# A two-batch transformer block on one core: where the q and k scales are made, when GpSimd scales the last residual, and which engines normalise the last tiles

## Time and profile before

| | |
|---|---|
| median of 3 executions | 521.55 us (521.29 to 521.72) |
| the profiled execution | 521.81 us, its span 519.7 us |
| mean granted TensorE clock | 0.998 of full speed |
| TensorE, busy | 501.1 us of the span (96%), 2976 matmuls |
| VectorE, busy | 413.0 us (79%) |
| ScalarE, busy | 405.5 us (78%) |
| GpSimd, busy | 255.7 us (49%) |
| DMA | 29.20 MB, mean 56 GB/s |
| chain that ended last, by engine | PE 79%, DVE 7%, POOL 5%, ACT 5%, issue 2%, DMA 1% |

### The profile page before, as it was taken

The page is one execution under the profiler, slowest core; times in us unless marked ns, Lnnn a source line. Parts: engine busy times, 40 slices in busy tenths (PEclk is TensorE's granted clock), DMA queues, the critical chain, the costliest instruction groups (busy, mean ns, idle before and its releaser), DMA issues.

```text
span 519.7 us, 8086 instructions
## 1 busy us (share of the span) xinstructions
PE 501.1 (96%) x2976; PEld 193.2 (37%) x2976; DVE 413.0 (79%) x705; ACT 405.5 (78%) x558; POOL 255.7 (49%) x295
## 2 busy tenths in 40 slices
PE   8899999999999999999999999999999999999994
PEld 3222222323222322234444444444444444444441
DVE  3699999989999997368878778778668666788677
ACT  1522888998899989877888888888888888888880
POOL 9100091823100715073464676664997962648741
PEclk9999999999999999999999999999999999999999
DMA  6410018576530005700031121140020020000022
GB/s 192 136 68 5 21 35 211 182 144 125 91 59 1 3 5 103 276 7 1 1 59 24 20 43 21 20 62 1 1 81 1 0 83 0 3 0 1 0 81 81
DMA packets 30151, 29.20 MB, mean 56 GB/s; under 512 B 19489, under 2 KB 21921, under 8 KB 29857
## 3 DMA queue, kind: packets, MB, share of 16 engines
q1 hardware_dynamic: 26688, 22.67, 15.7%
q0 software_dynamic: 3424, 6.03, 6.3%
HBM read 24.37 MB, written 4.23 MB: 55 GB/s over the span
## 4 chain that ended last, share of the span: by engine, by line
PE 79%; DVE 7%; POOL 5%; ACT 5%; issue 2%; DMA 1%; SPq 0%; DVEq 0%; POOLq 0%; ACTq 0%
PE ps L1123 16%; PE ps L1135 16%; PE ps L1157 16%; PE ps L1068 9%; PE ps L1039 6%; PE ps L963 6%; DVE mxh L1249 4%; ACT pbuf L760 3%; PE ps L892 3%; POOL x L617 2%; PE ps L1051 1%; PE ps L902 1%; PE ps L1016 1%; POOL stack L663 1%; DMA arena<-xT 1%
## 5 line engine op out<-in xcount | busy, mean ns | idle before, releaser
L1249 DVE TENSOR_REDUCE mxh<-ps 128x1 f32<-128x512 f32 x256 | 157.0, 680 | 6.5 <-PE ps L963 5.3
L760 ACT ACTIVATE pbuf<-ps,gamma 128x1024 f32<-128x1024 f32 x128 | 140.5, 1114 | 16.2 <-PE ps L1039 11.2
L841 ACT ACTIVATE ps<-ps,ratio 128x512 f32<-128x512 f32 x168 | 106.5, 659 | 40.4 <-PE ps L1123 37.3
L1157 PE MATMUL ps<-wd,stack 128*128 128x512 f16 x440 | 129.7, 379 | 0.7 <-POOL stack L663 0.6
L1123 PE MATMUL ps<-arena,wg 128*128 128x512 f16 x448 | 115.5, 379 | 0.1
L1135 PE MATMUL ps<-arena,wu 128*128 128x512 f16 x448 | 115.3, 379 | 0.1
L1423 DVE TENSOR_TENSOR ps<-ps,stack 128x512 f32<-128x512 f32 x128 | 87.8, 695 | 33.4 <-PE ps L1157 31.7
L847 ACT ACTIVATE ps<-ps,ratio 128x512 f32<-128x512 f32 x156 | 98.9, 659 | 6.6 <-PE ps L1135 2.3
L661 POOL CAST stack<-pbuf 128x512 f16<-128x512 f32 x55 | 33.5, 609 | 76.5 <-DVE pbuf L1398 76.5
L1423 DVE TENSOR_TENSOR ps<-ps,pbuf 128x512 f32<-128x512 f32 x76 | 52.6, 695 | 23.2 <-PE ps L1157 22.5
L1068 PE MATMUL ps<-pbuf,arena 128*32 128x256 f32 x832 | 66.5, 391 | 1.7 <-ACT avt L767 1.7
(11 more groups left out here) (120 smaller groups left out, 387.4 us busy)
## 6 DMA issues: line engine op xcount, KB each, us to landing
arena<-xT SPq DMA_DIRECT2D x16, 256.0 KB, 5.8
x<-x SPq DMA_DIRECT2D x2, 2048.0 KB, 10.0
out<-x SPq DMA_DIRECT2D x3, 1024.0 KB, 4.2
stack<-down_ratios SPq DMA_DIRECT2D x1, 2048.0 KB, 9.6
wg<-gq POOLq DMA_DIRECT2D x4, 448.0 KB, 7.3
wu<-uq POOLq DMA_DIRECT2D x4, 448.0 KB, 7.4
wd<-dq POOLq DMA_DIRECT2D x2, 896.0 KB, 10.3
pbuf<-down_ratios SPq DMA_DIRECT2D x1, 1536.0 KB, 6.2
```

Of the source, the lines that this page charges most:

```text
L760: nc.scalar.activation(pbuf[:, pi % 4, :].rearrange("p (a n) -> p a n", a=2), ps[:, at:at + 2, :], ACT.Exp, scale=gamma[:, n // (ALL // B) ...
L841: nc.scalar.activation(gbank[t % 2], gbank[t % 2], ACT.Copy, scale=gr[:, t % G, c:c + 1])\
L1157: mm = nc.tensor.matmul(bank[k], mparts[:, a, t % NM, k * P:(k + 1) * P], wd[:, i, :], start=(i == 0 and a == 0), stop=(a == 1), skip_grou ...
L1249: nc.vector.tensor_reduce(mxh[:, f % 2, qh, half:half + 1], ring_bank("first", n), AX.X, ALU.max)\
```

## The change

It has three parts.

1. *Scales.* For batch 0, VectorE takes the maxima straight from PSUM, before the bias is added, and adds the bias's absolute value to the combined maxima (a bound on the biased values instead of their maximum). ScalarE's eviction of a bank waits for VectorE's maxima of that bank. The maxima are turned by four matmuls that give the row on all 128 partitions at once (own kind first on each half), after the first value piece instead of the second; `scale_row` works on all partitions and writes `unit` and `gamma` itself, and `cast_scales` and `place_scales` go, for batch 1 as well, and with them one ring use. The first q rows are kept by VectorE instead of ScalarE. VectorE clears the first half of `vst` between the two maxima, GpSimd the second half after the low parts.
2. *Residual.* The ten multiplications stand at periods 26, 27, 33, 34, 35 and 40 to 44.
3. *The last tiles.* GpSimd negates the means of tiles 0 and 1; ScalarE subtracts them from PSUM and multiplies by the inverse deviation in a second instruction; it does that multiplication for tile 3 too, after VectorE has subtracted the mean, and issues that tile's store itself. VectorE does tile 2 whole.

```diff
-        row = sb("row", [1, 8], F32)
+        row = sb("row", [P, 4], F32)
...
-        TOPS_AT = {(2, 1): "tops", (4, 1): "cast"}
+        TOPS_AT = {(2, 1): "tops"}
...
-        RESIDUAL_AT = 28
+        RESIDUAL_AT = (26, 27, 33, 34, 35, 40, 41, 42, 43, 44)
...
-            for i, k in enumerate(LAST_ORDER):
+            def store_last(k):
                 t = BT * (NB - 1) + k
-                sp.wait_ge(s_res, BT * (NB - 1) + i + 1)
                 sp.dma_start(out[t], x1[:, t, :]).then_inc(s_out, 16)
+            for k in range(2):
+                sp.wait_ge(s_resa, k + 1)
+                store_last(k)
+            sp.wait_ge(s_res, BT * (NB - 1) + 1)
+            store_last(2)
...
+            pool.wait_ge(s_low, 2)
+            nc.gpsimd.memset(arena[:, 3, :], 0.0).then_inc(s_zero1, 1)
+            pool.wait_ge(s_zero1, 1)
+            nc.gpsimd.memset(vst[1][:, :, :, E:E + 1], float(HD) ** 0.5).then_inc(s_zero1, 1)
...
+            for k in range(2):
+                pool.wait_ge(s_st, 2 * NB + k)
+                nc.gpsimd.tensor_scalar(negm[:, k:k + 1], mv[:, k, 0:1], -1.0, None, ALU.mult).then_inc(s_neg, 1)
             inverse(2 * NB - 1, slice(0, 2), 2 * NB + 1)
             inverse(2 * NB, slice(2, 4), 2 * NB + 3)
...
-                act.wait_ge(s_proj, (1, 2, 4, 6)[2 * b + k])
+                if b == 0:
+                    act.wait_ge(s_top, k + 1)
+                else:
+                    act.wait_ge(s_proj, (4, 6)[k])
...
-                act.wait_ge(s_unit, 3)
+                act.wait_ge(s_projr, 2)
+                act.wait_ge(s_row, 4)
...
-            for n in range(3):
-                keep(n)
+            keep(0)
+            keep(2)
             project_v(0)
...
+            def centre(k):
+                act.wait_ge(s_neg, k + 1)
+                nc.scalar.activation(x1[:, (NB - 1) * BT + k, :], bank[k], ACT.Identity, bias=negm[:, k:k + 1])\
+                  .then_inc(s_cent, 1)
+            def scale_result(k):
+                x1_t = x1[:, (NB - 1) * BT + k, :]
+                act.wait_ge(s_rstd, 2 * NB + k // 2)
+                if k < 2:
+                    act.wait_ge(s_cent, k + 1)
+                else:
+                    act.wait_ge(s_cent3, 1)
+                nc.scalar.activation(x1_t, x1_t, ACT.Copy, scale=rstd[:, k:k + 1]).then_inc(s_resa, 1)
+            for k in range(2):
+                centre(k)
+            for k in (0, 1, 3):
+                scale_result(k)
+            act.wait_ge(s_resa, 3)
+            act.dma_start(out[NB * BT - 1], x1[:, NB * BT - 1, :]).then_inc(s_out, 16)
...
-                return [(qk, k, c) for k in range(2) for c in range(C)] + [(v, 0), (v, 1), (turn_tops, 0, bank[3]), (v, 2),
-                                                                           (cast_scales, 0, bank[3]), (v, 3), (vt,)]
+                return [(qk, k, c) for k in range(2) for c in range(C)] + [(v, 0), (turn_tops, 0, bank[3]), (v, 1), (v, 2),
+                                                                           (v, 3), (vt,)]
...
-                nc.tensor.transpose(dst[0:1, 0:P], tops[:, 2:3], ident[:]).then_inc(s_rf if b else s_turned, 1)
+                for own in range(2):
+                    for kind in range(2):
+                        at = HD * (kind != own)
+                        mm = nc.tensor.matmul(dst[own * HD:(own + 1) * HD, at:at + HD], tops[:, 2:3].to_broadcast([P, HD]),
+                                              ident[:, kind * HD:(kind + 1) * HD], start=True, stop=True)
+                mm.then_inc(s_rf if b else s_turned, 1)
...
-            nc.vector.memset(arena[:, 2:4, :], 0.0).then_inc(s_zero, 1)
...
+            def keep_first_q():
+                dve.wait_ge(s_put, 2)
+                nc.vector.tensor_copy(qs[0][:, 0, 0, :], put_bank(1)).then_inc(s_kept1, 1)
...
+                nc.vector.scalar_tensor_tensor(out=tops[:, 2:3], in0=tops[:, 0:1], scalar=tops[:, 1:2], in1=absb[:],
+                                               op0=ALU.max, op1=ALU.add).then_inc(s_topc, 1)
...
-                nc.vector.reciprocal(row[:, 4:6], row[:, 2:4]).then_inc(s_row, 1)
-                nc.vector.tensor_tensor(row[:, 6:7], row[:, 2:3], row[:, 3:4], ALU.mult).then_inc(s_row, 1)
+                nc.vector.reciprocal(unit[:, b:b + 1], row[:, 2:3]).then_inc(s_row, 1)
+                nc.vector.tensor_tensor(gamma[:, b:b + 1], row[:, 2:3], row[:, 3:4], ALU.mult).then_inc(s_row, 1)
...
-            for k in range(2):
-                row_maxima(0, k)
+            row_maxima(0, 0)
+            clear_first_v()
+            bias_magnitude()
+            row_maxima(0, 1)
             combine_tops(0)
             scale_row(0)
-            place_scales(0)
             low_parts()
+            keep_first_q()
...
-            for i, k in enumerate(LAST_ORDER):
-                x1_t = x1[:, (NB - 1) * BT + k, :]
-                dve.wait_ge(s_rstd, 2 * NB + i // 2)
-                nc.vector.tensor_scalar(x1_t, bank[k], mv[:, k, 0:1], rstd[:, k:k + 1], ALU.subtract, ALU.mult)\
-                  .then_inc(s_res, 1)
+            dve.wait_ge(s_st, 2 * NB + 3)
+            nc.vector.tensor_scalar(x1[:, NB * BT - 1, :], bank[3], mv[:, 3, 0:1], None, ALU.subtract).then_inc(s_cent3, 1)
+            dve.wait_ge(s_rstd, 2 * NB + 1)
+            nc.vector.tensor_scalar(x1[:, NB * BT - 2, :], bank[2], mv[:, 2, 0:1], rstd[:, 2:3], ALU.subtract, ALU.mult)\
+              .then_inc(s_res, 1)
```

More of the change, by code:

```diff
@@ L121, in build @@
         ident = sb("ident", [P, P], F32)
+        absb = sb("absb", [P, 1], F32)
         mhalf = sb("mhalf", [P, BT], F32)
@@ L153, in build @@
         s_bqk = sem("qk_bias_loaded")
+        s_absb = sem("qk_bias_magnitude_ready")
+        s_zero1 = sem("second_v_zeroed")
         s_wv = sem("v_weights_loaded")
@@ L227, in build @@
         s_lastw = sem("last_tile_weights_and_row_scaled")
+        s_neg = sem("last_means_negated")
+        s_cent = sem("last_tiles_centred_by_act")
+        s_cent3 = sem("last_tile_centred_by_dve")
+        s_resa = sem("last_results_by_act")
         s_res = sem("result_ready")
@@ L262, in wait_ring_read @@
                 engine.wait_ge(s_row, 6)
-            elif kind == "cast":
-                engine.wait_ge(s_unit, 6)
             else:
@@ L757, in exps @@
                 act.wait_ge(s_scf, pi + 1)
+                if pi == 0:
+                    act.wait_ge(s_row, 5)
                 if n >= 2 and pair == 0:
@@ L924, in turn_tops @@
                     pe.wait_ge(s_id, 2)
-                nc.tensor.transpose(dst[0:1, 0:P], tops[:, 2:3], ident[:]).then_inc(s_rf if b else s_turned, 1)
-            def cast_scales(b, dst):
-                pe.wait_ge(s_row, 5 * (b + 1))
-                if b == 0:
-                    pe.wait_ge(s_pick, 1)
-                nc.tensor.matmul(dst[:, P:P + 3], onerow[:], row[0:1, 4:7], start=True, stop=True)\
-                  .then_inc(s_rf if b else s_cast, 1)
+                for own in range(2):
[4 more added lines that the diff above has]
+                mm.then_inc(s_rf if b else s_turned, 1)
             def put(n):
@@ L955, in first_pass @@
                 if b == 0 and k == 0 and qt == 0 and jj == 0:
-                    pe.wait_ge(s_kept, 3 * t + 2 + half)
+                    pe.wait_ge(s_kept, 3 * t + 1 + half)
+                    pe.wait_ge(s_kept1, 1)
                 elif n == H * BT * 2:
@@ L979, in ring_use @@
                     turn_tops(n, ring_bank(kind, n))
-                elif kind == "cast":
-                    cast_scales(n, ring_bank(kind, n))
                 else:
@@ L1033, in scores @@
                     pe.wait_ge(s_vc, 2 * B)
-                    pe.wait_ge(s_kept, len(placed))
+                    pe.wait_ge(s_kept, len(placed) - 1)
+                    pe.wait_ge(s_kept1, 1)
                 else:
@@ L1186, in _, with clear_first_v, bias_magnitude @@
             nc.vector.memset(mhalf[:], -0.5).then_inc(s_const, 1)
-            nc.vector.memset(arena[:, 2:4, :], 0.0).then_inc(s_zero, 1)
-            dve.wait_ge(s_zero, 1)
-            for b in range(B):
-                nc.vector.memset(vst[b][:, :, :, E:E + 1], float(HD) ** 0.5)
-            def row_maxima(b, k):
-                dve.wait_ge(s_projr, (1, 2, 4, 6)[2 * b + k])
-                nc.vector.tensor_reduce(tops[:, k:k + 1], qkf[:, k * TB:(k + 1) * TB], AX.X, ALU.max,
-                                        apply_absolute_value=True).then_inc(s_top, 1)
+            def clear_first_v():
+                nc.vector.memset(arena[:, 2, :], 0.0).then_inc(s_zero, 1)
+                dve.wait_ge(s_zero, 1)
+                nc.vector.memset(vst[0][:, :, :, E:E + 1], float(HD) ** 0.5)
+            def bias_magnitude():
+                dve.wait_ge(s_bqk, 16)
+                nc.vector.tensor_reduce(absb[:], bqk_s[:], AX.X, ALU.max, apply_absolute_value=True).then_inc(s_absb, 1)
+            def row_maxima(b, k):
+                if b:
+                    dve.wait_ge(s_projr, (4, 6)[k])
```

(30 more changed lines are left out.)

29 lines of the change are left out of this document (13 added, 16 removed).

## The result

The changed kernel takes 517.75 us in the median (517.67 to 518.09, 4 executions) against 521.54 for the kernel before (521.29 to 521.72, 4 executions): ratio 0.9929, 95% interval 0.9912 to 0.9946, or -3.8 us. The forecast was 519.0 with a range of 517.9 to 520.5. The profiled execution took 517.72 us, its span 515.9.

What follows compares the result with a forecast made beforehand. TensorE, busy 96% of the span, bounds the kernel, leaving 18.6 us of gaps. Start -1.2, second batch's scales -0.2, residual -1.0 and tail -0.15 make -2.55: 521.81 to 519.26, median 519.0, range 517.9 to 520.5.

Steps and rivals of the forecast that it cites:

- The turn's price: Start, first batch: four fp32 matmuls replacing one 0.27 us turn take 0.9 us (0.64 to 1.1), so +0.63 us.
- the maxima: Start: VectorE takes the second maxima without waiting for ScalarE's eviction, at 13.55 instead of 14.27, -0.72 us.
- the cast and copies: Start: with cast and three copies removed, high parts wait for the reciprocal alone, 16.43 instead of 17.56; predicted -1.06 us.
- copying the first q rows: Start: VectorE instead of ScalarE copies them, so the first pass starts at 21.16 against 21.22, -0.06 us.
- the half clearing under cover: Start: clearing half the value buffer between the two maxima, 10.9 to 12.7 us, is free before the second maxima at 13.55.
- a tie: Start: three value pieces free TensorE at 17.9 to 18.3, placing is due at 18.17; up to 0.15 us against the change.
- The second batch's scales: Second batch: cast and VectorE copies go, the turn grows by 0.6; -0.2 us, between -0.6 and +0.3.
- The residual: Feed-forward part: moving ten multiplications closes TensorE's gaps of 0.73 and 0.29 us; -1.0 us, between 0 and -1.0.
- The tail: Last four tiles: transfers are saturated, so only the first store's earlier issue counts; -0.15 us.
- The issue-bound rival: Tail: a second queue adds throughput, so the tail gives -0.95 and the total -3.35, 518.2 us; chance 0.12.
- the rival of the eaten start: Start: turn at 1.1, value pieces and lockstep leave 0 to -0.5; total some -1.6, 519.9 to 520.4 us; chance 0.16.
- the moved stall: Feed-forward part: the residual's new places give nothing; total -1.55, 520.0 us; chance 0.07.
- the ring's phase: First passes after the fifth step take other ring banks; losing 0.07 us a step makes +1.5, 523.1 us; chance 0.04.

Runs made afterwards that it cites:

- quarter stores: Kernel before and changed kernel, each of the last four stores cut to 128 of 512 columns: last tile's first matmul to span's end 9.90 and 9.29 us.

## Why the prediction was wrong in size

- *The turn's price* is the step that failed most. It was put at 0.9 us, between 0.64 and 1.1, and measured 0.46. Both ends were wrong: the upper took the distance of two cast instructions, the lower one eighth of a 512-column instruction, 0.054; one more costs 0.031. Eight such with 0.2 us of tail are the row's 0.46. The argument from the 0.287 of the earlier trace rows (eight instructions, four transposes of v, not placings) took a row that carries its own tail for a price of issue, and nothing of a bound by weight loads showed at that size. This is 0.44 of the error, and V-P came out at -1.51 for -1.13 (with +0.06 from small things).
- *The rest of the relay* held: -0.71 for the maxima (predicted -0.72), -0.98 for the cast and copies (from the reciprocal's start to the high parts; predicted -1.06, and read from the two traces alone, as no run put the first cast back), nothing for copying the first q rows (P-F -0.02 for -0.06), the half clearing under cover (from 10.71; with the bias's size VectorE is free at 12.72, 0.36 us before the second maxima). Three value pieces behind the turn left 0.20 us to the placing, where a tie was feared.
- *The second batch's scales* measured -0.57 for -0.2. The wrong step was the balance "cast less turn, in a stretch where VectorE is the later". The turn's growth was absorbed and the cast's removal was not, because the cast is also a use of the ring; its wait of 0.27 was on the row of the prediction (0.21 idle) and was not counted. -0.6 was its lower bound, for the wrong reason: VectorE's copies were named, and they cost nothing.
- *The residual* came out at -1.0, as worked out from the two gaps, with the late cast 3.05 us earlier where 2.4 was worked out.
- *The tail* came out at -0.22 in the two traces, -0.19 alone, for -0.15. Reading the transfers instead of the issues was right: whole stores hide 0.38 of the gain. The issue-bound rival (-0.95) falls, and it would have overstated even with cheap transfers, where -0.60 was measured.
- *Nothing was foreseen* before the value projection (-0.32 in the means, part of it perhaps chance) and outside the span (medians 2.04 before, 1.93 after). These 0.4 us are not explained.

Sum by measured stretches: -1.51 - 0.04 - 0.57 - 1.00 - 0.22 = -3.3, and 0.4 from the last point is -3.8 when nothing is rounded. With the forecast's median the first sum alone is 518.2, inside the range; three errors, the turn's price, the ring's wait and the part not foreseen, of some 0.4 us each, pointed the same way. That -0.57 lay within the bounds of its term was luck, as said above. The range's lower end took the best ends of start and tail but not of the second batch (-0.6); with it the end is some 517.5. And the rival of the eaten start, by its own sum (a start of 0 to -0.5), gives 519.7 to 520.2 and not 519.9 to 520.4. Of the rivals, the eaten start, the moved stall and the ring's phase did not occur: in S-T nothing shifted but the cast's 0.57.

## What to carry to other kernels

Cut two traces at the same events before you explain a difference: here each stretch repeats to 0.08 us, several times better than the time itself, and a single execution can price an edit of 0.2 us. A small operation that goes through a ring of buffers costs its wait for the slot as well as itself, so count the slot when it is removed; and move a producer earlier only together with the place of its consumer in the next engine's queue (0.71 us here, of which 0.62 hang on the queue). At a tail of stores look at the transfer rate first: a last issue 0.9 us sooner brought 0.2.

## What the runs showed that was not expected

- Eight fp32 instructions with 64 stationary and 64 moving columns, four on each half of the array, follow each other at 0.031 us, where an eighth of the 0.43 us of a 512-column one is 0.054.
- VectorE's small instructions take as long on 128 partitions as on one (a reduction of 128 columns 0.29 for 0.28, the others 0.16 to 0.17 for 0.15 to 0.16), so a value can be made where it is needed instead of being spread.
- Two stores issued 0.09 us apart by ScalarE and SyncE landed in 2.5 and 2.7 us, where SyncE's stores 0.6 to 0.7 us apart landed in 2.0 to 2.2 (quarter stores: 1.8 and 1.9, for 1.6). The end came no sooner than with all four from SyncE.
- The start of the value projection, for which the first loads must have landed, has a standard deviation of 0.36 us over the twenty traces; no later stretch differs by more than 0.08 us between kernels that are alike in it.
